# GpSimd waits for its scatters to land behind every fourth one in place of every sixteenth

## The chip, the cores and the metric

One core of one Trainium2 chip runs the kernel. The metric is the device time of one execution, in microseconds (us).

## What is computed

Four rounds of message passing over a graph of 12500 nodes with 32 features each and 412500 edges, sorted by target. In the reference's words, shortened:

```python
edge_index = jnp.stack([src, dst])
x = _layernorm(x + _L0(x, src, dst))            # segment_sum(x[src], dst)
x = _layernorm(x + _L1(x, edge_attr_32, ...))   # segment_sum(relu(x[src] + edge_attr), dst), two small dense layers
x = _layernorm(x + _L2(x, src, dst, edge_weight, weight))   # segment_sum over rows of x[cols] * vals, times a matrix
x = _layernorm(x + _L3(x, edge_index, ...))     # segment_sum(norm * sigmoid(gate) * x[src], dst)
```

Layer 0 uses neither `edge_attr_32` nor `edge_weight`; layers 1 and 2 do.

## The kernel before

The edges are cut into 52 chunks (`NCH`) of 128 x 62 edges (`EC = P * G`). Nodes are laid out as 98 rows (`HB`) of 128. Gathers and sums are matmuls against one-hot matrices, which VectorE makes.

**The sort** comes first. For each chunk, TensorE counts (lines 1409, 1419, 1420), and VectorE (`rank_chunk`, line 765) works out a slot for every edge by its source node. It writes the slots into `idx` (line 790) and counts up `ranked`. `move` (line 1426) brings the targets into the same order, and ScalarE stores them in `row_table`.

**The scatters.** Layer 1 needs each edge's features, and layer 2 its weight, in slot order. SyncE loads a chunk's records from DRAM into `recs` (`load_recs`, line 428), in four spans of its 62 columns and a load of the weights. GpSimd (`scatter_chunk`, line 641) waits until the chunk is ranked, loaded and its slot table zeroed, copies indices and weights (lines 648, 649), and issues 62 indirect DMAs (line 652). Each writes 128 records of 33 words, one from each partition, to 128 rows of `slot_table` in DRAM, and adds 16 to `scattered` when it has landed. The loop:

```python
for g in range(G):
    pool.indirect_dma_start(
        out=slot_dram[c.number], out_offset=bass.IndirectOffsetOnAxis(ap=idx_now[:, c.slot, g:g + 1], axis=0),
        in_=recs[:, c.slot, g, :], in_offset=None).then_inc(scattered[c.slot], 16)
    if g % RUN == RUN - 1:
        pool.wait_ge(scattered[c.slot], 16 * (G * c.turn + g + 1))
    if g + 1 in (16, 32, 48):
        pool.sem_inc(spent, 1)
```

`spent` lets SyncE load the next records over the columns that have been read (line 431); the last span waits for `scattered` (line 433). `recs` holds two chunks. In all there are 52 x 62 = 3224 scatters.

**Layer 0** (`sum_sources`, lines 952, 1246, 1521) begins when the sort is over, beside the scatters that are left. It works through 52 x 10 = 520 blocks of 10 groups of 128 slots (the last block of a chunk has 8). Per block VectorE makes `hot_t` (line 929) and `hot_d` (line 919), TensorE gathers (line 1525, one weight load and one matmul per group), ScalarE copies the rows to `msg` (line 1254) and loads the next `lo_bc` (line 1235), and TensorE adds up (line 1516, again a weight load and a matmul per group). It reads nothing from `slot_table`.

**Layer 1** (`sum_edges`) reads `slot_table`: before a chunk's first block ScalarE waits until all 62 of its scatters have landed (line 1276). Layers 2 and 3 follow. None of them uses GpSimd.

Each engine has its own instruction queue, written out in the order of the code; semaphores join them.

Of the kernel before, what the change touches and what calls it, by code (L numbers as in the profile page):

```python
# [29 lines left out]
TILE = 125  # L30
QUAD = 4
FILLS = 16
RUN = 16
SPANS = ((0, 16), (16, 32), (32, 48), (48, 62))
BATCH = 8

# [39 lines left out]
def build_program(nc, x, src, dst, edge_attr, edge_weight, eps, w1, b1, w2, b2, w_lin, w_src, w_tgt,  # L76
# [29 lines left out]
    with ExitStack() as ctx:  # L106
# [515 lines left out]
        def _(pool):  # L622
# [18 lines left out]
            def scatter_chunk(c, loads):  # L641
# [9 lines left out]
# [6 lines that stand above are left out]
# [1020 lines left out]
```

## Time and profile before

| | |
|---|---|
| median of 3 runs | 11638.95 us (11632.47 to 11648.19) |
| the profiled execution: its own time | 11615.17 us |
| its span | 11613.4 us |
| busy: TensorE, VectorE, ScalarE, GpSimd | 52%, 58%, 35%, 32% |
| the sort | up to 1323 us |
| scatters | 89 to 5142 us |
| layer 0 | 1405 to 5994 us |
| layer 1 | 6150 to 7880 us |

In the rows, PE is TensorE's matmuls and PEld its weight loads, DVE is VectorE, ACT ScalarE, POOL GpSimd and SP SyncE. L652 is line 652 of the kernel. The words in brackets behind a row are the idle time of the engine before it and what ended it: "DMA" is a transfer that landed, "remote" something that the profile can't name, "issue" that the engine waited for nothing visible. The windows table gives for each stretch its length, then busy us and, in brackets, instructions of PE, PEld, DVE, ACT and POOL, then the granted clock of TensorE as a share of 2.4 GHz, the share of time that the DMA engines were busy, and GB/s.

### The profile page before, as it was taken

To read this page: it belongs to the slowest core of one execution; us is meant where nothing else is said; L and a number is where in the kernel's file an instruction comes from. 1 tells how busy PE (TensorE), PEld (TensorE's weight loads), DVE (VectorE), ACT (ScalarE), POOL (GpSimd) and SP (SyncE) were. 2 spreads that over 40 slices of the span, in tenths; PEclk is the share of its full clock that TensorE was granted. 3 is DMA by queue.
4 is the path that set the end of the run, shared out by engine and by line. 5 is a ranking of instruction groups with operands and counts; after the bars stand their busy time and mean duration, and the time that the engine had idled before them with its cause. 6 is when DMAs were issued, how large, how long until landed. Compare 5 with 4: busy or idle time off the path is not lost.

```text
span 11613.4 us, 288892 instructions
## 1 busy us (share of the span) xinstructions
PE 5989.1 (52%) x120824; PEld 5480.6 (47%) x120824; DVE 6785.5 (58%) x8337; ACT 4030.2 (35%) x6116; POOL 3672.4 (32%) x3346
## 2 busy tenths in 40 slices
PE   5777500000000000029976666666666666688886
PEld 5666400000000000028865656666666666688886
DVE  8999700000000000029978888886777777888895
ACT  2333200000000000015535555554888888233331
POOL 6778876676766666650000000000000000000000
PEclk8888755555555555569988888886666676799997
DMA  6554111111111111125536555553555554455552
GB/s 115 95 100 70 34 31 30 29 32 29 31 30 32 30 30 30 29 59 170 170 102 199 191 192 192 192 195 119 187 186 184 186 187 172 131 169 168 169 169 81
DMA packets 1123616, 1319.69 MB, mean 114 GB/s; under 512 B 581317, under 2 KB 869253, under 8 KB 1122183
## 3 DMA queue, kind: packets, MB, share of 16 engines
q1 hardware_dynamic: 716445, 572.55, 19.0%
q10 hardware_dynamic: 302952, 675.90, 17.5%
q0 software_dynamic: 103168, 54.68, 2.2%
q8 instruction: 970, 15.89, 0.6%
q14 instruction: 81, 0.66, 0.0%
HBM read 902.26 MB, written 400.43 MB: 112 GB/s over the span
## 4 chain that ended last, share of the span: by engine, by line
another core or an unknown queue 29%; DVE 23%; ACT 16%; issue 13%; PE 8%; ACTq 4%; DVEq 4%; DMA 3%; SPq 0%
ACT far_now L1322 9%; DVE hot_d L919 8%; ACT near_now L1285 4%; DMA source_marks<-near_now 3%; PE banks L1516 2%; PE banks L1426 2%; DVE hot_r L793 2%; DVE hot_t L929 2%; DVE left L1067 2%; DVE msg_z L1075 2%; ACT msg_z L1314 1%; DVE moved L772 1%; DVEq L796 1%; PE banks L1451 1%
## 5 line engine op out<-in xcount | busy, mean ns | idle before, releaser
L652 POOL DMA_INDIRECT slot_table<-recs,idx_now x3224 | 3611.3, 1120 | 1409.1 <-issue 960.1
L919 DVE TENSOR_TENSOR hot_d<-lodl,banks 128x2560 bf16<-128x2560 bf16 (+1 forms) x884 | 1487.1, 1682 | 1830.8 <-remote 1626.6
L1516 PE MATMUL banks<-hot_d,msg 128*96 128x256 bf16 x10192 | 1624.5, 304 | 1654.7 <-issue 1127.8
L1516 PEld LDWEIGHTS banks<-hot_d,msg 128*96 128x96 bf16 x10192 | 1237.6, 134 | 1803.0 <-issue 1264.5
L1254 ACT CAST msg<-banks 128x480 bf16<-128x480 f32 (+1 forms) x1040 | 522.2, 554 | 4103.2 <-remote 3260.0
L929 DVE TENSOR_SCALAR hot_t<-lo_bc,part_col 128x1280 bf16<-128x1280 bf16 (+1 forms) x884 | 529.1, 599 | 1774.2 <-remote 1379.4
L1525 PE MATMUL banks<-parts,hot_t 128*128 128x96 bf16 x5096 | 330.9, 217 | 2314.6 <-issue 1852.8
L1525 PEld LDWEIGHTS banks<-parts,hot_t 128*128 128x128 bf16 x5096 | 287.2, 103 | 2433.7 <-issue 2417.7
L1322 ACT CAST far_now<-hot_td 128x1792 fp8e4<-128x1792 bf16 x728 | 1187.8, 1679 | 34.3 <-DVE hot_td L937 33.5
L1570 PE MATMUL banks<-x_win,hot_td 128*128 128x32 bf16 x30576 | 881.9, 184 | 210.4 <-issue 193.6
L1570 PEld LDWEIGHTS banks<-x_win,hot_td 128*128 128x128 bf16 x30576 | 837.9, 101 | 227.4 <-issue 213.4
L1285 ACT CAST near_now<-hot_t 128x1792 fp8e4<-128x1792 bf16 x364 | 613.5, 1685 | 593.2 <-DMA source_marks<-near_now 400.7
L1604 PE MATMUL banks<-parts,near 128*128 128x33 bf16 x15288 | 688.6, 179 | 108.0 <-issue 100.4
L1604 PEld LDWEIGHTS banks<-parts,near 128*128 128x128 fp8e4 x15288 | 680.9, 96 | 120.7 <-issue 113.8
L919 DVE TENSOR_TENSOR hot_d<-lodl,iota_d 128x3584 bf16<-128x3584 bf16 x364 | 732.9, 2013 | 0.0
L1516 PE MATMUL banks<-hot_d,msg_z 128*96 128x256 bf16 x5096 | 684.3, 286 | 50.8 <-DVE msg_z L1075 26.0
L1607 PE MATMUL banks<-b_win,dl_bc 128*128 128x3 bf16 x10192 | 674.5, 164 | 41.4 <-issue 41.4
L1581 PE MATMUL banks<-msg_z,hot_d 128*128 128x32 bf16 (+1 forms) x15288 | 461.8, 183 | 368.9 <-DVE msg_z L1023 368.6
L1607 PEld LDWEIGHTS banks<-b_win,dl_bc 128*128 128x128 fp8e4 x10192 | 622.6, 96 | 43.5 <-issue 43.5
L1516 PEld LDWEIGHTS banks<-hot_d,msg_z 128*96 128x96 bf16 x5096 | 584.3, 127 | 79.7 <-DVE msg_z L1075 67.0
L1581 PEld LDWEIGHTS banks<-msg_z,hot_d 128*128 128x128 bf16 x15288 | 434.0, 101 | 394.1 <-DVE msg_z L1037 384.8
L937 DVE TENSOR_SCALAR hot_td<-dl_bc,part_col 128x1792 bf16<-128x1792 bf16 x728 | 466.6, 683 | 262.1 <-ACT far_now L1322 249.1
(183 smaller groups left out, 9748.4 us busy)
## 6 DMA issues: line engine op xcount, KB each, us to landing
lo_bc<-row_table ACTq DMA_DIRECT2D x364, 448.0 KB
dl_bc<-row_table SPq DMA_DIRECT2D x364, 448.0 KB, 4.3
target_marks<-far_now ACTq DMA_DIRECT2D x364, 448.0 KB, 3.5
dl_bc<-target_marks SPq DMA_DIRECT2D x364, 448.0 KB, 4.2
lo_bc<-row_table ACTq DMA_DIRECT2D x468, 320.0 KB
slot_table<-zeros SPq DMA_DIRECT2D x52, 1617.0 KB, 11.6
rec_in<-slot_table ACTq DMA_DIRECT2D x364, 231.0 KB, 2.7
source_marks<-near_now ACTq DMA_DIRECT2D x364, 224.0 KB, 2.3
```

Source lines behind the costliest of these rows:

```text
L652: pool.indirect_dma_start(out=slot_dram[c.number], out_offset=bass.IndirectOffsetOnAxis(ap=idx_now[:, c.slot, g:g + 1], axis=0), in_=recs[ ...
L919: v.tensor_tensor(hot[:, blk.slot, 0:half], ids.unsqueeze(2).to_broadcast([P, half, WIN, 2]), steps.unsqueeze(1).to_broadcast([P, half, WI ...
L929: v.tensor_scalar(hot_t[:, blk.slot, 0:blk.n * P], lo_bc[:, blk.across], part_col[:, 0:1], None, ALU.is_equal).then_inc(hot_t_made[q], 1)
L1254: s.copy(msg[:, blk.slot, 5 * j:5 * j + n, :].rearrange("p g f -> p (g f)"), banks[:, 2 * blk.slot + j, 0:3 * D * n]).then_inc(taken[0], 1)
L1285: s.copy(near_now[:, :].bitcast(F8), hot_t[:, blk.slot, :], saturate=False).then_inc(near_kept, 1)
L1322: s.copy(far_now[:, blk.slot, k * (BG * P // 2):(k + 1) * (BG * P // 2)].bitcast(F8), hot_td[:, blk.slot, k, :], saturate=False).then_inc( ...
L1516: mm = t.matmul(banks[0:3 * D, 6 + blk.par, 0:WIN], rows[:, blk.slot, g, :], hot[:, blk.slot, g // 2, :, g % 2], start=(blk.b == 0 and g = ...
L1525: mm = t.matmul(banks[:, 2 * blk.slot + g // 5, 3 * D * (g % 5):3 * D * (g % 5 + 1)], hot_t[:, blk.slot, slots_of(blk, g)], parts[:, blk.h ...
L1570: mm = t.matmul(banks[:, 7, D * g:D * g + D], hot_td[:, blk.slot, k, slots_of(blk, g)], x_win[:, blk.par, k, q * D:(q + 1) * D], start=(k ...
L1581: mm = t.matmul(banks[:, blk.b, at:at + cols], hot_s[:, blk.slot, g // 2, :, g % 2], msg_z[:, blk.slot, g, first:end], start=False, stop=F ...
L1604: t.matmul(banks[:, blk.slot, at:at + YA], near8[:, kept_of(blk, g)], parts3[:, blk.h0 + g, q, :], start=(q == 0), stop=(q == 2))
L1607: mm = t.matmul(banks[:, blk.slot, at + YA:at + 36], hot_far[:, blk.b, k, slots_of(blk, g)], b_win[:, blk.par, k, 0:3], start=(k == 0), st ...
```

## The change

One constant is smaller, and with it the number of scatters between two waits in `scatter_chunk`. The waits before stood behind the 16th, 32nd and 48th scatter of a chunk; now they stand behind the 4th, 8th, 12th and so on up to the 60th. `spent` is counted up at the same places as before.

```diff
 TILE = 125
 QUAD = 4
 FILLS = 16
-RUN = 16
+RUN = 4
 SPANS = ((0, 16), (16, 32), (32, 48), (48, 62))
 BATCH = 8
```

## Rows read from the trace of the kernel before

**Rows 1.** The page: the span.

```profile
span 11613.4 us, 288892 instructions
```

**Rows 2.** Windows table by stage: busy us and instructions of each engine, granted clock, DMA share.

```profile
0.00:1323.00 1323.00, 923.58 (x12876) 828.22 (x12876) 1205.30 (x793) 453.92 (x985) 1012.95 (x541) 0.86 0.48 85
...
1524.00:5092.00 3568.00, 286.25 (x1332) 149.28 (x1332) 141.53 (x144) 68.56 (x137) 2474.73 (x2634) 0.50 0.15 30
...
5152.00:5994.00 842.00, 764.14 (x8708) 693.56 (x8708) 830.54 (x932) 448.07 (x891) 0.00 (x0) 1.00 0.53 166
...
6150.00:7880.00 1730.00, 1153.48 (x19777) 1055.58 (x19777) 1503.51 (x1820) 1005.81 (x1416) 0.00 (x0) 0.86 0.59 191
```

**Rows 3.** Section 4 of the page, the chain that ended last.

```profile
another core or an unknown queue 29%; DVE 23%; ACT 16%; issue 13%; PE 8%; ACTq 4%; DVEq 4%; DMA 3%; SPq 0%
```

**Rows 4.** GpSimd's waits, 0 to 1323 us: released by, us in total, times, longest.

```profile
POOL slot_table L652 <- DMA slot_table<-recs,idx_now: 103.5, 24, 10.8
```

**Rows 5.** The scatters (line 652), 0 to 1323 us: count, ns min/median/max.

```profile
L652 POOL DMA_INDIRECT slot_table<-recs,idx_now x505: 956/962/5058, 89.0 to 1322.8; - x169
```

**Rows 6.** GpSimd's waits, 1405 to 5142 us.

```profile
POOL slot_table L652 <- DMA slot_table<-recs,idx_now: 234.7, 120, 2.0
POOL slot_table L652 <- remote: 97.5, 19, 7.6
```

**Rows 7.** The scatters (line 652), 1405 to 5142 us.

```profile
L652 POOL DMA_INDIRECT slot_table<-recs,idx_now x2676: 955/962/1287, 1405.2 to 5140.8; - x192
```

**Rows 8.** Timeline of GpSimd around one wait: start us, us, operation, idle before.

```profile
2411.06 0.96 POOL L652 DMA_INDIRECT slot_table<-recs,idx_now  x1 [0.30 <-issue]
2414.01 0.96 POOL L652 DMA_INDIRECT slot_table<-recs,idx_now  x1 [1.99 <-DMA slot_table<-recs,idx_now]
```

**Rows 9.** Timeline of TensorE and VectorE in one block of layer 0.

```profile
2368.48 1.49 DVE L919 TENSOR_TENSOR hot_d<-lodl,banks 128x2560 bf16<-128x2560 bf16 x1 [20.55 <-remote]
...
2370.30 0.63 PE L1516 MATMUL banks<-hot_d,msg 128*96 128x256 bf16 x2
...
2392.86 0.37 PE L1516 MATMUL banks<-hot_d,msg 128*96 128x256 bf16 x1 [3.12 <-issue]
...
2424.49 1.49 DVE L919 TENSOR_TENSOR hot_d<-lodl,banks 128x2560 bf16<-128x2560 bf16 x1 [27.35 <-remote]
```

**Rows 10.** Line 919 on VectorE, one per block: 1404 to 5150 us, then 1524 to 5092 us.

```profile
L919 DVE TENSOR_TENSOR hot_d<-lodl,banks x75: 1220/1489/1490, 1404.7 to 5148.5; 128x2560 bf16<-128x2560 bf16 x68, 128x2048 bf16<-128x2048 bf16 x7
...
L919 DVE TENSOR_TENSOR hot_d<-lodl,banks x69: 1220/1489/1490, 1524.3 to 5091.8; 128x2560 bf16<-128x2560 bf16 x62, 128x2048 bf16<-128x2048 bf16 x7
```

**Rows 11.** The same, 5154 to 5994 us.

```profile
L919 DVE TENSOR_TENSOR hot_d<-lodl,banks x445: 1207/1476/1487, 5153.8 to 5991.2; 128x2560 bf16<-128x2560 bf16 x134, 128x2048 bf16<-128x2048 bf16 x15
```

**Rows 12.** Timeline around the last scatter.

```profile
5140.75 0.96 POOL L652 DMA_INDIRECT slot_table<-recs,idx_now  x1 [0.30 <-issue]
...
5148.45 1.49 DVE L919 TENSOR_TENSOR hot_d<-lodl,banks 128x2560 bf16<-128x2560 bf16 x1 [28.25 <-remote]
...
5153.83 1.48 DVE L919 TENSOR_TENSOR hot_d<-lodl,banks 128x2560 bf16<-128x2560 bf16 x1
```

**Rows 13.** Timeline, a pause of GpSimd at a chunk's start and the blocks after it.

```profile
3588.79 0.98 POOL L652 DMA_INDIRECT slot_table<-recs,idx_now  x1 [5.62 <-remote]
...
3592.21 1.49 DVE L919 TENSOR_TENSOR hot_d<-lodl,banks 128x2560 bf16<-128x2560 bf16 x1 [19.20 <-remote]
...
3618.22 1.49 DVE L919 TENSOR_TENSOR hot_d<-lodl,banks 128x2560 bf16<-128x2560 bf16 x1 [8.72 <-remote]
```

**Rows 14.** Timeline of VectorE's line 919 around a second such pause.

```profile
4620.74 1.49 DVE L919 TENSOR_TENSOR hot_d<-lodl,banks 128x2560 bf16<-128x2560 bf16 x1 [27.55 <-remote]
...
4676.74 1.49 DVE L919 TENSOR_TENSOR hot_d<-lodl,banks 128x2560 bf16<-128x2560 bf16 x1 [27.55 <-remote]
...
4731.34 1.49 DVE L919 TENSOR_TENSOR hot_d<-lodl,banks 128x2560 bf16<-128x2560 bf16 x1 [26.15 <-remote]
```

**Rows 15.** That pause, on GpSimd.

```profile
4627.17 0.98 POOL L652 DMA_INDIRECT slot_table<-recs,idx_now  x1 [6.70 <-remote]
```

## The prediction

> **What bounds the kernel now.** I read the span [rows 1], the table of windows by stage, the chain, then GpSimd's waits and the timelines. [Rows 2] split the run into stages. Up to 1323 us VectorE is busy for 1205 of 1323 us: it ranks the edges, and GpSimd scatters beside it. From 1524 to 5092 us the only engine that works steadily is GpSimd (2475 of 3568 us, nearly all of it scatters); TensorE, VectorE and ScalarE are busy for under 10% and TensorE is at its lower clock, 0.50 or 1.2 GHz. From 5152 us, with no scatter left, the same code of layer 0 runs with TensorE busy for 764 and VectorE for 831 of 842 us, at a granted clock of 1.00. The chain puts 29% of the span down to "another core or an unknown queue" [rows 3]; that is this middle stretch.
>
> What holds layer 0 there? It reads nothing that the scatters write. Line 919 on VectorE runs once per block, and layer 0 has 52 x 10 = 520 blocks. [Rows 10]: 75 of them start between 1404.7 and 5148.5 us, and 68 steps from 1524.3 to 5091.8 make 52.5 us per block. [Rows 11]: the other 445 take 1.89 us each (842/445), 28 times faster. [Rows 9] show a slow block: TensorE issues a few matmuls of line 1516 at once and then one per 2 to 3 us, and VectorE's next 919 comes 56.0 us after the last. With 20 matmuls and 20 weight loads in a block, that is 1.4 us per instruction. [Rows 12] show the end of it: the last scatter is issued at 5140.75, line 919 still comes late at 5148.45, and the one after that at 5153.83. The slow blocks end some 8 to 12 us after the last scatter. So the path is: GpSimd's scatters until 5141.7, about 10 us, then the rest of layer 0 at 1.89 us a block, then all other layers. **A microsecond more of scattering is a microsecond more of kernel**, less what TensorE gets done in it.
>
> **What the change does.** It removes nothing and moves nothing. The 62 scatters of a chunk had waits behind the 16th, 32nd and 48th; now behind the 4th, 8th, up to the 60th: 15 in place of 3, so 12 x 52 = 624 waits are added. Queued behind each is the next scatter on GpSimd, nothing else but the chunk's two copies. Those who wait for GpSimd are SyncE's loads of later records (by `spent` and `scattered`), which are freed by the same scatters and have two chunks of slack, and layer 1's first loads, long after.
>
> **Price of a wait, undisturbed.** A scatter follows the last one after 0.30 us, and after a wait after 1.99 us [rows 8]; over the stretch, 234.7 us in 120 waits is 1.96 us [rows 6]. The difference is 1.66 us. The scatters after it aren't shorter for it (0.96 us both ways, [rows 8]; the median is 962 ns, [rows 7]), so nothing is won back. From 1405 to 5142 us there are 2676 scatters, 1.396 us each with all waits; 12/62 x 1.66 = 0.321 us more makes 1.717.
>
> **Price beside the ranking.** Up to 1323 us, 24 waits took 103.5 us [rows 4], 4.3 us each, 4.0 over the plain gap. The 505 scatters [rows 5] from 89 us on took 1234 us, 2.24 us each without the waits. At 15/62 waits of 4.0 us each (2.24 + 0.97 = 3.21 us) only 384 get done in that time: 121 are left for later, at 1.717 us each, 208 us. At 1.66 us a wait, 59 are left, 101 us. VectorE sets this stage and doesn't wait for GpSimd, so nothing else moves here. The upper end has the row of this very stage, but its mean is carried by waits of up to 10.8 us, and some scatters there last up to 5.1 us [rows 5] behind VectorE, time that a wait could cover; I take 177.
>
> The Trainium skill ("SBUF — State Buffer", the box on the trap that VectorE blocks a DMA) says that GpSimd can't write descriptors while VectorE holds the shared ports in a two-port mode. By that, pauses there are partly free and the lower end would hold; the long scatters in this trace agree with the lock.
>
> **The later stretch.** 3224 - 505 = 2719 scatters x 0.321 = 873 us. Together 873 + 177 = 1050 us; ends 974 and 1081. The last scatter then ends near 6190 us.
>
> **What TensorE gets done meanwhile.** The slow stretch grows from 3743 to some 4793 us. At 52.5 us a block, 1050/52.5 = 20 more blocks are done in it, which the tail is spared: 20 x 1.89 = 38 us. Do the added pauses speed the blocks? The block of 56.0 us in [rows 9] has two such waits in it, one of them in [rows 8], and lasts as long as 20 pairs of 2.8 us: they gave it nothing. Longer pauses, at a chunk's start, do sometimes: after one of 5.62 us the next step is 26.0 us [rows 13]. After another of 6.70 us [rows 15] the next steps are 56.0 and 54.6 [rows 14]. There are 19 such pauses, 97.5 us in all [rows 6]. So: blocks at 52.5 us as now; bounds 56 us (19 blocks, 35 us saved) and 20 us (240 blocks done in the slow stretch, not 75: 312 us saved).
>
> Sum: 1050 - 38 = +1012 us. The profiled execution took 11615 us, so 12627; the median of the runs shown is 24 us above it, so **12650 us**. Ends: 974 - 312 gives 12300; 1081 - 35 and a pause of 5.1 us (97.5/19) at the other 33 chunk starts too, 168 us, gives 12850.
>
> **Rivals.** *TensorE is not slowed down any more* (faster). Its place is layer 0 from 1405 us. After the last scatter the slowness is gone within 12 us [rows 12], and the first blocks after 1405 were still fast. If the slowness builds up under dense scatters and drains in pauses, then 4 scatters in 5 us and 2 us of rest (0.6 per us, now 0.72) may never fill it; next to the ranking, at 505 in 1234 us (0.41 per us), TensorE was busy for 924 of 1323 us [rows 2]. For it: [rows 13]. Against: [rows 9, 14, 15]. Then layer 0 takes about 983 us and ends near 2400. Layer 1, 1730/52 = 33 us a chunk [rows 2], is paced by scatters at 62 x 1.717 = 106 us a chunk; it ends some 35 us after the last one (6190, or 460 later if 983 us go at the 3.2 us per scatter of the ranking stage), and what now follows 7880 us takes 3735. That is 9960 to 10420, say 10200. The point from which it decides: the tail has only 445 x 1.89 = 841 us to give, so layer 0 must be over 209 us before the last scatter for layer 1 to pay the rest: 4580/520 = 8.8 us a block or less, six times faster than now. Anything short of that stays slower than before. Chance 0.18.
>
> *TensorE's slowness has nothing to do with the scatters* (no change). Then layer 0 speeds up at 5152 us by a cause of its own; layer 1 starts at 6150 and needs the last chunk only 1700 us later, with the last scatter at 6190. The time stays at 11640. Against: [rows 12]. Chance 0.02.
>
> The Trainium skill ("SBUF — State Buffer", "Who interferes with whom") states: "PE and ACT never wait on anyone." By that rule scatters can't hold TensorE and 11640 would be the time; the trace speaks against it, since a block goes from 56.0 to 1.89 us right where they end.
>
> *Blocks get faster, but not enough*: at 20 us a block, 11639 + 1050 - 312 = 12380 us; inside the range, 0.08.
>
> **The numbers.** My forecast has 0.72 and its faster-block variant 0.08, all slower by far more than the 0.2% (23 us) that a measurement of this kernel can tell; faster 0.18, same 0.02. The range of 12300 to 12850 covers the forecast, its bounds and the variant; the faster rival is left out.
>
> **What the new profile would show.** Right: 156 waits become 780, at 1.96 us from 1405 us on; fewer than 505 scatters before 1323 us (384 to 446); the last scatter near 6190; some 95 blocks of layer 0 before it, 52 us each; every stage after it as long as now. Wrong: blocks of a few us while scatters still run, or waits far from 2 us.

## The result, and the profile after

The change takes 10220.47 us, median of 4 runs (10202.07 to 10229.19). The kernel before, measured beside it, takes 11643.57 us, median of 4 (11632.47 to 11652.01). The ratio is 0.8776 [0.8761 to 0.8791]: 12% faster, where 12650 us was forecast. The profiled execution took 10202.07 us. On another chip of the same type the same change is 13% slower; that is the main finding of the experiments.

The page of the kernel after: its span, and its chain that ended last.

```profile
span 10200.3 us, 288892 instructions
...
ACT 12%; DVE 12%; issue 7%; PE 4%; ACTq 2%; DMA 1%; DVEq 0%; SPq 0%
```

These shares add up to 38%: followed back, this chain ends at 6409 us, at the last scatter, and doesn't say what came before. So it can't be compared with [rows 3], where the chain reaches back to the start and 29% is "another core or an unknown queue". What changed earlier stands in the windows table of the kernel after (columns as in [rows 2]: window, its length, busy us and instructions of PE, PEld, DVE, ACT and POOL, granted clock, DMA share, GB/s).

```profile
0.00:1323.00 1323.00, 916.16 (x12876) 817.81 (x12876) 1204.23 (x793) 445.20 (x985) 817.23 (x414) 0.87 0.47 82
1405.00:2400.00 995.00, 811.32 (x8978) 715.11 (x8977) 876.81 (x961) 451.03 (x916) 529.47 (x548) 0.98 0.65 166
4000.00:5000.00 1000.00, 279.17 (x3864) 243.14 (x3864) 296.69 (x355) 194.15 (x275) 577.13 (x609) 0.59 0.32 84
```

The second of these windows, of the kernel before:

```profile
1405.00:2400.00 995.00, 90.07 (x432) 48.80 (x430) 45.76 (x47) 21.11 (x42) 693.71 (x739) 0.50 0.17 33
```

In the same 995 us TensorE executes 8978 matmuls in place of 432, beside 548 instructions of GpSimd in place of 739. Layer 0 is over while the scatters go on. The lines that tell it are line 1254 on ScalarE, which runs twice per block of layer 0, line 976 on VectorE, which runs once per batch of layer 1, and line 652, the scatters. They give count, duration ns min/median/max, and first and last start; kernel after:

```profile
L1254 ACT CAST msg<-banks x1040: 405/565/593, 1395.2 to 2520.0; 128x480 bf16<-128x480 f32 x174
...
L976 DVE TENSOR_TENSOR total<-banks,rec_in x364: 609/624/626, 2632.5 to 6461.5; 128x448 f32<-128x448 f32 x182
...
L652 POOL DMA_INDIRECT slot_table<-recs,idx_now x3224: 952/958/5067, 90.5 to 6409.4; - x190
```

Kernel before:

```profile
L1254 ACT CAST msg<-banks x1040: 404/560/566, 1403.2 to 5991.7; 128x480 bf16<-128x480 f32 x174
...
L976 DVE TENSOR_TENSOR total<-banks,rec_in x364: 611/618/627, 6102.5 to 7879.0; 128x448 f32<-128x448 f32 x182
```

Layer 0 takes 1125 us, 2.16 us a block (520 blocks), where it took 4589. It ends at 2520 instead of 5992. Layer 1 then runs behind the scatters and ends 52 us after the last of them, at 6461 in place of 7879; all that follows takes 3739 us in place of 3734.

GpSimd's waits in the kernel after (released by, us in total, times, longest), from 0 to 1323 us, from 1405 to 5142 us, and in the whole run:

```profile
POOL slot_table L652 <- DMA slot_table<-recs,idx_now: 355.9, 92, 11.4
```

```profile
POOL slot_table L652 <- DMA slot_table<-recs,idx_now: 1189.2, 498, 5.6
```

```profile
POOL slot_table L652 <- DMA slot_table<-recs,idx_now: 1925.2, 778, 11.4
```

The waits do cost time: 2.39 us each in the later stretch, against 1.96 before [rows 6], and 3.87 us beside the ranking. The last scatter starts 1269 us later than before (6409.4 against 5140.8). The kernel is faster because TensorE is held far less: all of layer 0 and nearly all of layer 1 now run beside the scatters.

### The profile page after: what moved, and what is told of

It reads as the page before. It is cut to its first block and busy times, and to the rows that moved or that the text cites. A ratio compares the mean times of both kernels' runs of the same rounds, so it can differ in the third digit from the quotient of the medians.

```text
span 10200.3 us, 288892 instructions
## 1 busy us (share of the span) xinstructions
PE 6048.7 (59%) x120824; PEld 5568.7 (55%) x120824; DVE 6804.8 (67%) x8337; ACT 4015.0 (39%) x6116; POOL 3673.9 (36%) x3346
## 5 line engine op out<-in xcount | busy, mean ns | idle before, releaser
L1516 PE MATMUL banks<-hot_d,msg 128*96 128x256 bf16 x10192 | 1667.3, 322 | 2032.9 <-DVE msg L996 1676.4
L1516 PEld LDWEIGHTS banks<-hot_d,msg 128*96 128x96 bf16 x10192 | 1353.5, 145 | 2170.8 <-DVE msg L996 1670.9
L996 DVE TENSOR_TENSOR msg<-left,msg 128x448 bf16<-128x448 f32 x364 | 225.7, 620 | 1641.8 <-ACT msg L1298 944.3
L1544 PEld LDWEIGHTS banks<-parts,hot_t 128*128 128x128 bf16 x15288 | 441.2, 100 | 567.2 <-DVE hot_t L929 390.0
L1544 PE MATMUL banks<-parts,hot_t 128*128 128x32 bf16 x15288 | 472.6, 182 | 468.5 <-DVE hot_t L929 322.0
L976 DVE TENSOR_TENSOR total<-banks,rec_in 128x448 f32<-128x448 f32 x364 | 226.5, 622 | 629.3 <-remote 564.6
```

The lines of the kernel that those rows point to most:

```text
L1516: mm = t.matmul(banks[0:3 * D, 6 + blk.par, 0:WIN], rows[:, blk.slot, g, :], hot[:, blk.slot, g // 2, :, g % 2], start=(blk.b == 0 and g = ...
L1544: mm = t.matmul(banks[:, blk.slot, D * g:D * g + D], hot_t[:, blk.slot, slots_of(blk, g)], parts[:, blk.h0 + g, q, :], start=(q == 0), sto ...
```

## The experiments

**Theories**, by the letters that the expectations use. B: dense scatters fill something that slows TensorE, and rests of any kind drain it. C (in e2 and e11 it is called rival D): landing matters; a wait for it keeps few scatters unconfirmed, and that relieves TensorE. E: only the start of layer 0 can tip over; an engine that is once fast stays fast. F: the chip that a run lands on decides whether scatters slow TensorE. G: chip and mean density of the scatters decide together. Two more have no letter: that the slowness, once full, stays, and that it has no link with the scatters. The kernels ran on whichever chip was free; its number is told with each result. That of the chip of the first measurement is not on record.

### Between the two kernels, and past them

e1_run8 has a third of the added waits (7 in a chunk in place of 15, before 3), e3_run2 more than twice as many (31), e4 the added waits only until chunk 18.

```diff
-RUN = 4
+RUN = 8          # e1_run8;  e3_run2: RUN = 2
```
```diff
 # e4_run4_to_chunk18, with RUN = 16 in place of 4 from chunk 18
+                    run = 4 if c.number < 18 else 16
-                    if g % RUN == RUN - 1:
+                    if g % run == run - 1:
```

> GpSimd waits behind every eighth scatter: 7 waits a chunk in place of 3 (before) or 15 (the change), bursts of 8 scatters (10 us) with 2 us of rest. Theory B (build-up): TensorE is slowed by something that dense scatters fill and a rest drains; a burst of 8 is short enough only if the filling is slower than 2 us of draining per 10 us. If so, a chunk costs 62 x 1.27 + 7 x 1.7 = 90 us against 106 with waits behind every fourth, the last scatter falls near 5600 us and the kernel takes 9300 to 9600 us. If a burst of 8 already fills it, layer 0 is slowed again and the kernel takes 12000 us or so (before + 4 x 52 x 1.66 = 345 us). Rival C (landing): TensorE is fast as soon as few scatters are in flight; 2 us after each scatter it has landed either way, so 8 would act like 4: 9300 to 9600 us as well.

> Waits behind every second scatter: 30 a chunk (behind the 62nd too it is 31), a chunk costs 62 x 1.27 + 31 x 1.7 = 131 us. Theory B and all others that have the change's gain from an unslowed TensorE: still fast, and bound by the scatters: 16 x 52 x 1.7 = 1400 us more than the change, 11400 to 11900 us. If the gain had come from the waits in another way (the more the better), below 10200 us.

> Waits behind every fourth scatter for chunks 0 to 17, whose scatters cover the ranking and layer 0; from chunk 18 on behind every sixteenth. Theory B (build-up): dense scatters come back when layer 1 is running, TensorE is slowed to 1.4 us an instruction there, 98 x 3 + 98 matmuls and as many weight loads make a chunk of layer 1 some 1000 us, so that layer 1 stands still until the last scatter (near 5600 us) and then takes most of its 1730 us: about 5600 + 1600 + 3735 = 10900 to 11000 us. Rival E (only the start of layer 0 can tip over; an engine that is once fast stays fast): a chunk costs 86 us, the last scatter falls near 5700 us and the kernel takes 9400 to 9500 us.

e2_rest_by_memset keeps the waits behind every 16th scatter; at the other places where the change waits, GpSimd clears a small tile of its own four times, about 1.3 us in which no scatter is issued and no landing is waited for.

```diff
-RUN = 4
+RUN = 16
...
                     if g % RUN == RUN - 1:
                         pool.wait_ge(scattered[c.slot], 16 * (G * c.turn + g + 1))
+                    elif g % 4 == 3:
+                        for _ in range(4):
+                            pool.memset(rest_of_pool[:, :], 0.0).then_inc(rested, 1)
+                            rests[0] += 1
+                            pool.wait_ge(rested, rests[0])
```

> Waits for landing stay behind the 16th, 32nd and 48th scatter as before; behind the 4th, 8th, 12th and so on of the others GpSimd rests without waiting for a scatter, by four small memsets in a row that each wait for their own semaphore (some 2 us in all). Theory B (build-up, a matter of rest): as with the change, layer 0 at 2 us a block, 10200 us give or take 400 by the length of the rest. Rival D (the wait for the landing itself matters, since it keeps at most 4 scatters unconfirmed): layer 0 stays at some 52 us a block and the kernel takes about 12600 us, before plus the rests.

All four ran on chip 12, and the expectations had no such case: there the kernel before takes 9093.41 us (median of 7), not 11640. Against it: e1 9468.14 us, 1.042 [1.040 to 1.044]; e2 9689.87, 1.066 [1.063 to 1.069]; e3 11339.67, 1.248 [1.244 to 1.251]; e4 9604.69, 1.056 [1.054 to 1.059]. All are slower, and among those that only add waits (e1, e4, e3), the more the slower. e1 lies in its expected range of 9300 to 9600 us, but that says nothing of B, since on this chip layer 0 is fast without any added wait (1.9 us a block in all four). So before anything could be said of the change, the chips had to be told apart.

### The same two kernels on another chip

e5_before_again is the kernel before, e6_change_again the change; no edit.

> The kernel before, once more with a profile. In the last call it took 9093 us, not 11640. Theory F (a condition of the place): whether scatters slow TensorE in layer 0 depends on the chip or core that a run lands on, the kernel is the same. Where it took 9093 us, layer 0 must run at 2 us a block beside the scatters and end near 2500 us, 52 chunks of scatters at 84 us pace layer 1, and the last scatter falls near 5300 us. Where it takes 11640 us, the profile is that of before: 75 blocks up to 5150 us.

> The change, timed beside before where this call lands. Theory F: where before takes 9093 us, the change only adds 12 x 52 waits to a run that the scatters pace anyway: + 624 x 1.66 us = 1036 us and a little more, 10150 to 10250 us, 12% slower than before. Where before takes 11640 us, the change takes 10220 us as first measured. Rival (the first measurement's gain holds everywhere): the change is 12% below before in any case, 8000 us here.

On chip 11 e5 took 9100.75 us and the kernel before beside it 9104.38 (7 runs). e6 took 10265.71 us: 1.1275 [1.1252 to 1.1297] **slower**. Layer 0 on this chip in the kernel before, then in the change:

```profile
L1254 ACT CAST msg<-banks x1040: 405/558/592, 1388.8 to 2375.9; 128x480 bf16<-128x480 f32 x174
```

```profile
L1254 ACT CAST msg<-banks x1040: 405/558/592, 1390.5 to 2372.4; 128x480 bf16<-128x480 f32 x174
```

Both need 1.9 us a block, with and without the added waits. The windows row of the kernel before on chip 11 against the one shown above, the same program on the first chip:

```profile
1405.00:2400.00 995.00, 900.96 (x10120) 819.26 (x10118) 962.83 (x1075) 515.23 (x1025) 676.35 (x710) 0.99 0.73 186
```

GpSimd issues nearly as much in both (710 and 739 instructions), and TensorE is busy for 901 us here and for 90 us there. So there are two kinds of place: some on which this kernel slows TensorE down, and some on which it doesn't. By the number on record they are told as affected and unaffected chips; only chip 12 was met at two different times, so that it is the chip, and not something else that went on there at that time, is not shown. Here the added waits show their bare price; GpSimd's waits and the scatters in e5, then in e6:

```profile
POOL slot_table L652 <- DMA slot_table<-recs,idx_now: 510.3, 155, 10.3
...
L652 POOL DMA_INDIRECT slot_table<-recs,idx_now x3224: 952/958/5307, 90.4 to 5309.0; - x190
```

```profile
POOL slot_table L652 <- DMA slot_table<-recs,idx_now: 1958.4, 778, 11.0
...
L652 POOL DMA_INDIRECT slot_table<-recs,idx_now x3224: 952/958/5085, 90.2 to 6475.5; - x190
```

The last scatter starts 1166 us later, and the kernel takes 1161 us longer; e6 lies 16 us above its expected range.

### Fewer waits than before

e7_run32_two_spans waits once in a chunk, e8_no_waits never within one. The loads of later records are freed span by span (`spent`), so the spans had to be made longer with it.

```diff
-RUN = 4
-SPANS = ((0, 16), (16, 32), (32, 48), (48, 62))
+RUN = 32                       # e8: RUN = 64
+SPANS = ((0, 32), (32, 62))    # e8: SPANS = ((0, 62),)
...
-                    if g + 1 in (16, 32, 48):
+                    if g + 1 == 32:             # e8: never
                         pool.sem_inc(spent, 1)
```

> One wait a chunk, behind the 32nd scatter, and two spans of records in place of four. Theory F, where before takes 9100 us: between before and no waits: 2 x 52 waits of 3.3 us less 0.3 us go away, 310 us: 8800 us. Where before takes 11640 us, TensorE is slowed as in before or worse and the time is 11350 to 11500 us. Theory B is dead where scatters without any wait ran beside an unslowed layer 0; if this one is slowed where before is not, it would be back.

> No wait behind any scatter. So that SyncE may load new records only once the old ones have landed, a chunk's records come in one load that waits for all scatters of two chunks earlier. Theory F, where before takes 9100 us: the scatters pace the kernel, and 156 waits at 3.3 us (510.3 us in 155) less the 0.30 us of the plain gap go away, 465 us: 8640 us, if a load of all 62 columns is still in time. Theory B (dense scatters fill something): with no rest at all TensorE is slowed even here, layer 0 falls back to 20 to 56 us a block, and the kernel takes 11300 us or more. Where before takes 11640 us, both expect 11200 to 11400: the last scatter 260 to 465 us earlier, layer 0 as slow as before.

e7, on chip 12: 8841.17 us against 9120.97, 0.969 [0.966 to 0.972]. e8, on chip 14: 8686.13 against 9128.55, 0.952 [0.950 to 0.954]. Layer 0 and the scatters beside it in e8:

```profile
L1254 ACT CAST msg<-banks x1040: 405/558/567, 1393.4 to 2384.0; 128x480 bf16<-128x480 f32 x174
...
L652 POOL DMA_INDIRECT slot_table<-recs,idx_now x774: 954/958/1498, 1392.0 to 2383.9; - x194
```

Both came near the 8800 and 8640 us expected. In e8 0.78 scatters start per us, and a block still takes 1.9 us. Density alone, whatever the chip, is refuted.

With 3, 7, 15 and 31 waits in a chunk, and 1 or none, the unaffected chips give a price per wait: the change adds 12 x 52 = 624 waits for 1161 us, 1.86 us each; e1 adds 208 for 375 us, 1.80; e3 adds 28 x 52 = 1456 for 2246 us, 1.54; e8 takes 156 away and wins 442 us, 2.8 each, with the loads of records changed along with it. e4 adds 216 waits for 511 us, 2.37 each; some 74 of them lie beside the ranking (384 scatters start before 1323 us), and most others beside layer 0. e2's rests cost 0.96 us each (597/624).

### Thin the scatters in the middle of layer 0

e9_run4_from_chunk14 has the kernel before up to chunk 13 and the change from chunk 14.

```diff
-RUN = 4
+RUN = 16
...
+                    run = 16 if c.number < 14 else 4
-                    if g % RUN == RUN - 1:
+                    if g % run == run - 1:
```

> The reverse of e4: waits behind every sixteenth scatter for chunks 0 to 13, behind every fourth from chunk 14 on. Theory G (place and density together): where before takes 9100 us, TensorE is never slowed and only the added waits count: 38 chunks x 12 x 2.2 us (e6: 1958 us in 778 waits against 510 in 155; 1448/623 = 2.3, less the 0.3) = 900 to 950 us, 10000 us. Where before takes 11640 us, layer 0 starts slowed and is let go within some 100 us after the scatters thin out at chunk 14 (1405 + about 5 chunks x 88 = 1850 us), so layer 0 ends near 2900 and the kernel takes 10050 to 10200 us, again bound by the scatters. If it stays slowed (once tipped over, always slowed), 12400 us.

It ran on chip 3, where the kernel before takes 11616.38 us: an affected one. It took 9884.95 us, 15% less (one run each) and 165 us below the 10050 to 10200 expected. GpSimd's timeline where chunk 14 begins (start us, us, operation, idle before); in this kernel the lines from 656 on have a number one higher:

```profile
1855.46 0.28 POOL L649 COPY recs<-w_now 128x62 f32<-128x62 f32 x1
1861.40 0.98 POOL L652 DMA_INDIRECT slot_table<-recs,idx_now  x1 [5.66 <-remote]
...
1865.21 0.96 POOL L652 DMA_INDIRECT slot_table<-recs,idx_now  x1 [0.30 <-issue]
1867.61 0.96 POOL L652 DMA_INDIRECT slot_table<-recs,idx_now  x1 [1.44 <-DMA slot_table<-recs,idx_now]
```

VectorE's step per block beside it:

```profile
1552.49 1.49 DVE L920 TENSOR_TENSOR hot_d<-lodl,banks 128x2560 bf16<-128x2560 bf16 x1 [27.35 <-remote]
1608.49 1.49 DVE L920 TENSOR_TENSOR hot_d<-lodl,banks 128x2560 bf16<-128x2560 bf16 x1 [27.55 <-remote]
...
1826.97 1.49 DVE L920 TENSOR_TENSOR hot_d<-lodl,banks 128x2560 bf16<-128x2560 bf16 x1 [27.58 <-remote]
1877.38 1.49 DVE L920 TENSOR_TENSOR hot_d<-lodl,banks 128x2560 bf16<-128x2560 bf16 x1 [21.95 <-issue]
1907.69 1.49 DVE L920 TENSOR_TENSOR hot_d<-lodl,banks 128x2560 bf16<-128x2560 bf16 x1 [7.38 <-remote]
1914.96 1.49 DVE L920 TENSOR_TENSOR hot_d<-lodl,banks 128x2560 bf16<-128x2560 bf16 x1 [1.07 <-PE banks L1517]
1919.37 1.49 DVE L920 TENSOR_TENSOR hot_d<-lodl,banks 128x2560 bf16<-128x2560 bf16 x1 [0.35 <-PE banks L1517]
```

The steps are 56.0 us, then, from the thinning at 1861 on, 50.4, 30.3, 7.3 and 4.4 us. The 50.4 us are no sign yet: the same step, between the 11th and the 12th block, takes 51.1 us in the kernel before. The remaining blocks follow at a mean of 2.27 us (the first row below: 507 starts, 1149.8 us), beside 656 scatters in about the same time, 0.57 per us:

```profile
L920 DVE TENSOR_TENSOR hot_d<-lodl,banks x507: 1201/1478/1489, 1915.0 to 3064.8; 128x2560 bf16<-128x2560 bf16 x152, 128x2048 bf16<-128x2048 bf16 x17
...
L652 POOL DMA_INDIRECT slot_table<-recs,idx_now x656: 953/961/1482, 1914.5 to 3065.1; - x164
```

A full slowness is thus lifted within some 60 us by sparser scatters: "once full, it stays" is refuted, and so is "no link with the scatters", since nothing else is switched at 1861. The single pause of 5.66 us there isn't the reason, since after one of 5.62 us in the kernel before [rows 13] the steps are 26.0, 37.8, 53.9 and again 56.0 us. The granted clock follows: it is at its lower level (0.50, 1.2 GHz) from 1500 to 1850 us, where TensorE was busy for 27 of 350 us, and means 0.92 from 1900 to 2100. It is no explanation by itself: the two levels differ twofold, the blocks 25-fold.

### Between 4 and 16, and rests, on an affected chip

e10, e12 and e13 are e1's kernel again, e11 is e2's, e14 is e8's, until a run met an affected chip.

> Waits behind every eighth scatter, once more, to meet a chip on which before takes 11640 us. Theory G (place and density together): there the slowness built up over some 100 us at 0.72 scatters per us and went within 60 us at 0.58 (e9). Every eighth gives 0.66 to 0.7 per us beside layer 0, in between. If it stays below the threshold, layer 0 takes under 1500 us and the kernel 9450 to 9600 us; if it passes it, blocks of 20 to 56 us and 11300 to 12000 us. Where before takes 9100 us it takes 9470 us again.

> Waits behind every eighth scatter, a third try to meet a chip on which before takes 11640 us (so far chips 3 and 15; chips 7, 11, 12 and 14 gave 9100). A rest of 1.3 us in 6.1 us held there (e11, 0.66 scatters per us), one of 1.7 us in 22 us did not (before, 0.72). Every eighth rests 1.7 us in 11.8, 0.68 per us. Theory G, if the mean density decides: near the edge, layer 0 either at 2.5 to 4 us a block (kernel 9450 to 9700) or slowed (11300 to 12000). Where before takes 9100 us it takes 9470 us again.

> Waits behind every eighth scatter, where before takes 11640 us: near the edge (0.68 scatters per us): 9450 to 9700 us if layer 0 stays unslowed, 11300 to 12000 if not. Where before takes 9100 us: 9470 us.

> The rests by memsets once more, to meet a chip on which before takes 11640 us: waits for landing behind every sixteenth scatter, as before, and a rest of some 1.4 us behind the other fourth ones. Theory G: it is the mean density of scatters that counts, not the waiting: layer 0 runs fast and the kernel takes 9700 to 9900 us. Rival D (the wait for landing counts): layer 0 at 52 us a block, 12200 to 12600 us. Where before takes 9100 us it takes 9690 us again.

> No waits at all, where before takes 11640 us: scatters at 0.79 per us, denser than before, so layer 0 is slowed to 56 us a block or worse: last scatter near 4900 us, then 10 us, then 450 blocks at 1.89 us and 5620 us for the rest: 11350 to 11450 us. If density doesn't matter there, near 8700. Where before takes 9100 us: 8690 us.

e10 (chip 7: 9483.42 us, before 9108.47) and e12 (chip 5: 9456.29, before 9089.10) met unaffected ones and repeat e1's 4%. e13 met chip 1: 10785.25 us against 11628.69, 7% less. e14 ran there too: 11560.33, 0.6% less. e11 met chip 15: 9676.57 against 11602.76, 17% less. These are one run each. e11 came 23 us below its expected range, and e13 and e14 fit neither branch of theirs: 9450 to 9700 or 11300 to 12000 us for e13, 11350 to 11450 or 8700 for e14. The slowness is no switch but has sizes in between. Layer 0 in e13, in e11 (there line 1264) and in e14:

```profile
L1254 ACT CAST msg<-banks x1040: 405/559/592, 1402.8 to 4839.5; 128x480 bf16<-128x480 f32 x174
```

```profile
L1264 ACT CAST msg<-banks x1040: 405/565/594, 1392.5 to 2708.1; 128x480 bf16<-128x480 f32 x174
```

```profile
L1254 ACT CAST msg<-banks x1040: 405/558/592, 1417.0 to 5932.1; 128x480 bf16<-128x480 f32 x174
```

The scatters in the same time, in the same order (in e14 up to the end of the scatters), and last those of the change:

```profile
L652 POOL DMA_INDIRECT slot_table<-recs,idx_now x2358: 952/958/1463, 1402.2 to 4837.9; - x197
```

```profile
L657 POOL DMA_INDIRECT slot_table<-recs,idx_now x818: 953/959/1477, 1392.0 to 2707.8; - x164
```

```profile
L652 POOL DMA_INDIRECT slot_table<-recs,idx_now x2618: 952/958/1265, 1416.2 to 5069.0; - x187
```

```profile
L652 POOL DMA_INDIRECT slot_table<-recs,idx_now x597: 952/958/1472, 1395.2 to 2517.6; - x199
```

Each density is the count of such a row over its stretch; the blocks' means are from the rows above, for e14 and before from steps of line 919 ([rows 10]; 61 steps of 52.5 us in e14):

| affected chips | scatters per us beside layer 0 | us per block |
|---|---|---|
| the change | 0.53 (597 in 1122 us) | 2.16 |
| e9 from chunk 14 | 0.57 | 2.27 |
| e11, rests in place of waits | 0.62 | 2.5 |
| e13, RUN = 8 | 0.69 | 6.6 |
| before [rows 7] | 0.72 | 52.5 |
| e14, no waits | 0.72 | 52.5 |

C falls with e11: its waits for landings are those of the kernel before (155 in its trace, as in e5), its rests of about 1.3 us are shorter than the 1.96 us after which a landing was seen [rows 6], and its blocks are fast. GpSimd's waits in e11:

```profile
POOL slot_table L657 <- DMA slot_table<-recs,idx_now: 475.1, 155, 10.5
...
POOL slot_table L657 <- POOL rest_of_pool L664: 172.1, 620, 0.3
```

The table supports G: on affected chips the density orders all six, and the rise is steep between 0.62 and 0.72. Two things keep it from being a law. The burst, that is, the number of scatters in a row between two rests, orders them as well (4, 4, 4, 8, 16, 62), and no run has the same density with other bursts, but for before and e14, both at full slowness. And the density is in part an effect: where layer 0 is fast it takes time from the scatters. The kernel of e13 runs at 0.61 scatters per us beside the fast layer 0 of chip 12 (596 in 984 us in e1), and at 0.69 here.

e14 leaves a further doubt: with no wait at all it reaches no more scatters per us than before, since it pauses longer at the chunks' starts (the first row below; before it was 97.5 us, 19 times, [rows 6]). There the program has GpSimd wait for nothing but its own two copies (line 650). On an unaffected chip that takes 0.3 us each time (e5, the second row) and none of its 52 chunk starts has a longer pause; in e14 35 of them last over 2 us. So TensorE isn't the only engine that is held. Nothing above 0.72 was seen on such a chip.

```profile
POOL slot_table L652 <- remote: 259.5, 31, 11.9
```

```profile
POOL slot_table L652 <- POOL recs L649: 14.5, 52, 0.3
```

What holds, then: the place and how densely the scatters are issued decide together, with build-up and draining as in B; whether the mean or the length of a burst counts is open. On the unaffected chips no run slowed TensorE. E was not put to its test, since e4 met no affected chip. But e13 shows what B expected of it: layer 1 is slowed as well. While scatters still run, its first 29 batches come 14.8 us apart (28 steps in 414.6 us), where they come 4.9 us apart without scatters in the kernel before (364 of them from 6102.5 to 7879.0 us). This is e13 from 4839 to 5398 us:

```profile
L976 DVE TENSOR_TENSOR total<-banks,rec_in x29: 617/624/626, 4977.5 to 5392.1; 128x448 f32<-128x448 f32 x29
```

The affected chips show a trace of it even where nobody looked for it, in the ranking up to 1323 us. TensorE's waits at line 1419 "for nothing that the profile shows" (us in total, times, longest), from 100 to 1300 us, in e14, in e13 and in the change on the first chip:

```profile
PE banks L1419 <- issue: 75.5, 63, 3.1
```

```profile
PE banks L1419 <- issue: 32.0, 35, 2.4
```

```profile
PE banks L1419 <- issue: 13.7, 18, 1.7
```

In the kernel before it reads 68.2 us, and in e8, on an unaffected chip, 0.4 us, once. The dose follows the scatters here too (550, 459 and 382 of them before 1323 us, 505 in the kernel before). VectorE, which sets this stage, hides most of it: the first row of layer 0 starts at 1417.0 us in e14 and at 1393.4 in e8.

### Is one version best on both kinds?

| | affected | unaffected |
|---|---|---|
| before | 11603 to 11644 us | 9089 to 9129 us |
| no waits (e14, e8) | 11560 | **8686** |
| RUN = 8 (e13, e1) | 10785 | 9468 |
| the change | 10220 | 10266 |
| rests, no added waits (e11, e2) | **9677** | 9690 |

The rests beat the change on both kinds, because they cost half as much (0.96 us against 1.86) and suffice. The rows of e11, e13 and e14 are single runs, and the rests and the change met different affected chips. On unaffected chips the best is to wait for nothing.

## Why the prediction was wrong

**What bounds the kernel, and how it ends: half right.** That layer 0 was held by the scatters, and by nothing that it reads from them, was right: e9 and e13 show it. The sentence that a microsecond more of scattering is a microsecond more of kernel was wrong on the first chip, where the scatters ended 1269 us later and the kernel 1413 us earlier, because it needs the blocks to stay slow. On chip 11, where no block is ever slow, it holds (1166 us of scatters, 1161 us of kernel), there by way of layer 1, which needs the scatters.

**Price of a wait: right in kind, too small.** 1.96 us to the next scatter became 2.39 us in the later stretch, where more data moves beside it: 2.68 us beside layer 0 (DMA share 0.65 in the window shown, against 0.17 before) and 2.01 us from 4000 to 5000 us, at 0.32. It was 3.9 us in the ranking stage, near the 4.3 of [rows 4]. 1.717 us per scatter was forecast, and it was 3736/2061 = 1.81. The last scatter started at 6409 and not near 6190. 384 to 446 scatters before 1323 us were forecast, and it was 382: the upper price there was nearer. The 177 us taken for that stage has no working of its own; the 123 scatters left over (505 - 382) at 1.81 us make 223.

**What TensorE gets done meanwhile: the step that failed.** "Blocks at 52.5 us as now" gave 38 us for it; the trace of the change shows 2.16 us a block, all 520 blocks before the last scatter in place of 95, and nearly all of layer 1 too. In the terms of the sum (+1050 - 38) the spans give +1269 for the scatters and -2682 for the work done beside them. It rested on [rows 9, 14 and 15], single pauses of 2 to 7 us beside blocks of 56 us, which showed no effect. They lie in a stretch at 0.72 scatters per us, where the slowness is full; there one pause lowers the mean by next to nothing. What the change alters is the mean, 0.72 to 0.53, and with it the length of a burst, and the answer is steep: e13 gives 6.6 us at 0.69 and bursts of 8. Signs of something that fills and drains were at hand. [Rows 12] show 8 to 12 us of delay at the end, and at the start of layer 0 in the kernel before the steps grow, 9.9, 25.9, 30.1, 51.8 and 56.0 us; the prediction mentions these early blocks only in a rival:

```profile
1406.52 1.48 DVE L919 TENSOR_TENSOR hot_d<-lodl,banks 128x2560 bf16<-128x2560 bf16 x1
1416.41 1.49 DVE L919 TENSOR_TENSOR hot_d<-lodl,banks 128x2560 bf16<-128x2560 bf16 x1 [4.52 <-remote]
1442.35 1.49 DVE L919 TENSOR_TENSOR hot_d<-lodl,banks 128x2560 bf16<-128x2560 bf16 x1 [14.28 <-remote]
1472.48 1.49 DVE L919 TENSOR_TENSOR hot_d<-lodl,banks 128x2560 bf16<-128x2560 bf16 x1 [14.25 <-remote]
1524.28 1.49 DVE L919 TENSOR_TENSOR hot_d<-lodl,banks 128x2560 bf16<-128x2560 bf16 x1 [27.37 <-issue]
1580.29 1.49 DVE L919 TENSOR_TENSOR hot_d<-lodl,banks 128x2560 bf16<-128x2560 bf16 x1 [27.56 <-remote]
```

**The rival "not slowed down any more": right, at its own price.** 9960 to 10420 us was worked out, and 10220 measured. That it lies so near the 10200 is in part luck: the last scatter came 219 us after the 6190 of the lower end, about halfway to the 460 that the range allowed. Its other parts hold: layer 0 near 983 us (1125 measured), layer 1 ending some 35 us after the last scatter (52), 3735 us for the rest (3739). Its point of decision, 8.8 us a block, fits too: e13 lies below it at 6.6 and is 7% faster. It had 0.18, since the argument against it came from a stretch of full slowness, and the range left it out.

**The rival without any link** (11640 us) was rightly made small: e9 rules it out on affected chips. The rule of the Trainium skill that the prediction put beside it ("SBUF — State Buffer", "Who interferes with whom": PE never waits on anyone) stands in a section on the ports of SBUF. Taken for all that can hold TensorE, as the prediction took it, it is contradicted there by 56.0 us a block in the kernel before and by e9's thinning; whether the slowness goes by those ports at all, no run here shows. On chips 5, 7, 11, 12 and 14 the traces agree with it: 1.9 us a block at up to 0.78 scatters per us.

**"Faster, but not enough"**: not seen; with RUN = 8, on chip 1, even a third of the added waits suffices to be faster.

## What to carry to other kernels

Where an engine is slow beside another one's traffic, ask how its slowness answers to the mean rate of that traffic, and don't read the answer from a single pause inside a saturated stretch; onset and end of the slow stretch show whether it fills and drains. A first try is to thin the traffic by cheap rests of its own engine, not by waits for landings, which cost twice as much here. And measure on more than one chip: this change is 12% faster in one place and 13% slower in another, so that neither number alone says whether to keep it.

## What was not expected of the hardware

- Chips of the same type differ by some 27 to 28% on one kernel: 9089 to 9129 us on chips 5, 7, 11, 12 and 14, and 11603 to 11644 us on chips 1, 3, 15 and that of the first measurement. What makes them differ stays open, and so does whether a chip keeps its kind: chip 12 did over two measurements, and no affected chip was met at a second time.
- On the affected ones, dense indirect scatters of GpSimd hold TensorE to 1.4 us per instruction in layer 0 (56.0 us for 40), which reads nothing that they write. By what path is open as well; rests and waits both relieve it, so it goes by how densely the scatters are issued and not by waiting for their landing. GpSimd is held too, for up to 11.9 us at a chunk's start in e14.
- The waits for landings of the kernel before are themselves worth 5% on unaffected chips (e8, 442 us for 156 waits, 2.8 us each, more than the 1.66 us read from an undisturbed pair; the loads of records were changed along with them). Waits for the scatters four earlier, which might cost less, weren't tried.
